# A transformer layer on eight cores: layernorm squares given to GpSimd, and every other gate-weight cast to VectorE

## What is computed

```python
def attn(x):                     # 16 heads of 64
    q = phi(heads(x @ Wq.T + bq)); k = phi(heads(x @ Wk.T + bk))   # phi = elu + 1
    v = heads(x @ Wv.T + bv)
    kv = einsum('bhtd,bhtm->bhdm', k, v)
    z = 1.0 / (einsum('bhtd,bhd->bht', q, k.sum(axis=2) + EPS) + EPS)
    return (q @ kv * z) @ Wo.T + bo
def ffn(x):                      # hidden 3072, int32 weights times 1/127
    return (silu(x @ wg.T) * (x @ wu.T)) @ wd.T
x = layernorm(x + attn(x))
x = layernorm(x + ffn(x))
```

## Time and profile before

| | us |
|---|---|
| median of the two timed runs | 5167.56 |
| these runs | 5112.57 and 5222.55 |
| the profiled execution's time | 5038.7 |
| its span (core 2, the slowest; the eight are 5019.1 to 5037.2) | 5037.2 |
| TensorE busy | 3672.0 (73%) |
| VectorE busy | 1673.3 (33%) |
| ScalarE busy | 1295.7 (26%) |
| GpSimd busy | 29.8 (1%) |

### The profile page before, as it was taken

One profiled execution on the slowest core, in us unless ns is written; L12 is line 12 of the kernel. 1 busy time (PEld: TensorE's weight loads), 2 busy tenths in 40 slices (PEclk: granted clock), 3 DMA queues, 4 the chain that ended last, 5 costly groups with the idle time before them and its releaser, 6 DMA issues.

```text
span 5037.2 us, 43743 instructions; the slowest of 8 cores (5019.1 to 5037.2 us)
## 1 busy us (share of the span) xinstructions
PE 3672.0 (73%) x15184; PEld 1440.3 (29%) x15184; DVE 1673.3 (33%) x2411; ACT 1295.7 (26%) x2299; POOL 29.8 (1%) x52
## 2 busy tenths in 40 slices
PE   1577647777756866799965866699974877599992
PEld 0232213333312322244421322244431322144440
DVE  0113422223332134333333133333343134333334
ACT  2234421111132344211123244311113243411113
POOL 0000000000000000000000000000000000000000
PEclk9797668888878977899987977799996987799995
DMA  5100022222211000010102000010003000001001
GB/s 159 44 1 1 0 75 75 75 76 76 74 67 67 1 1 0 26 51 26 51 34 100 1 0 1 25 42 34 35 16 134 1 1 0 25 26 51 26 26 67
DMA packets 69677, 199.99 MB, mean 40 GB/s; under 512 B 4933, under 2 KB 4934, under 8 KB 60248
## 3 DMA queue, kind: packets, MB, share of 16 engines
q1 hardware_dynamic: 57656, 157.35, 9.0%
q10 hardware_dynamic: 11808, 39.85, 2.4%
HBM read 144.75 MB, written 52.43 MB: 39 GB/s over the span
## 4 chain that ended last, share of the span: by engine, by line
PE 58%; ACT 14%; DVE 13%; DMA 8%; issue 6%; POOL 1%; DVEq 0%; ACTq 0%; SPq 0%; POOLq 0%
PE ps L767 13%; PE ps L746 12%; PE ps L792 12%; PE ps L412 5%; PE ps L615 5%; PE ps L367 4%; DVE wstage L248 4%; DVE x L252 4%; DMA wstage_i<-wu 3%; DMA wstage_i<-wg 3%; ACT arena L187 2%; ACT arena L185 1%; ACT arena L537 1%; ACT arena L581 1%; DVE h_arena L778 1%
## 5 line engine op out<-in xcount | busy, mean ns | idle before, releaser
L746 PE MATMUL ps<-y_bf,arena 128*128 128x512 bf16 x3072 | 706.0, 388 | 141.7 <-POOL arena L715 95.8
L767 PE MATMUL ps<-y_bf,arena 128*128 128x512 bf16 x3072 | 704.9, 386 | 106.8 <-DVE arena L715 106.8
L792 PE MATMUL ps<-h_arena,arena 128*128 128x512 bf16 x3072 | 694.1, 379 | 35.5 <-DVE h_arena L778 35.5
L756 ACT ACTIVATE h_arena<-ps 128x512 bf16<-128x512 f32 x384 | 229.1, 597 | 1805.2 <-PE ps L746 1805.1
L778 DVE SCALAR_TENSOR_TENSOR h_arena<-ps,h_arena 128x512 bf16<-128x512 f32 x384 | 265.6, 692 | 1044.0 <-PE ps L767 1043.3
L804 DVE SCALAR_TENSOR_TENSOR x<-ps,x 128x512 f32<-128x512 f32 x768 | 530.7, 692 | 182.3 <-DVE x L804 91.1
L412 PE MATMUL ps<-wk_bf,arena 128*128 128x512 bf16 x1024 | 286.7, 428 | 299.3 <-ACT arena L435 179.4
L746 PEld LDWEIGHTS ps<-y_bf,arena 128*128 128x128 bf16 x3072 | 304.8, 99 | 529.6 <-issue 182.9
L767 PEld LDWEIGHTS ps<-y_bf,arena 128*128 128x128 bf16 x3072 | 303.5, 99 | 492.5 <-issue 143.4
L792 PEld LDWEIGHTS ps<-h_arena,arena 128*128 128x128 bf16 x3072 | 293.7, 98 | 420.2 <-issue 80.1
L524 PE MATMUL ps<-arena,wq_bf 128*128 128x512 bf16 x1024 | 283.9, 447 | 96.8 <-ACT arena L537 86.6
(11 more groups left out here) (78 smaller groups left out, 2445.6 us busy)
## 6 DMA issues: line engine op xcount, KB each, us to landing
x<-x SPq DMA_DIRECT2D x16, 2048.0 KB, 8.2
out<-x SPq DMA_DIRECT2D x16, 2048.0 KB, 7.7
arena<-stash_wg SPq DMA_DIRECT2D x18, 1024.0 KB, 5.0
arena<-stash_wd SPq DMA_DIRECT2D x18, 1024.0 KB, 7.2
arena<-stash_wu ACTq DMA_DIRECT2D x18, 1024.0 KB, 4.8
wstage_i<-wg SPq DMA_DIRECT2D x48, 256.0 KB, 3.1
wstage_i<-wd ACTq DMA_DIRECT2D x48, 256.0 KB, 2.9
wstage_i<-wu SPq DMA_DIRECT2D x48, 256.0 KB, 2.7
```

What stands on the lines that cost most here:

```text
L746: e.matmul(ps[b_][:, 0:512], slots[sl_][:, 512 * kk + 128 * gg:512 * kk + 128 * (gg + 1)], y_bf[:, T * kk + t_:T * kk + t_ + 512], start=( ...
L756: e.activation(h_arena[:, 512 * gg:512 * (gg + 1)], ps[b_][:, 0:512], AF.Silu, scale=S127), inc=act)
L767: e.matmul(ps[b_][:, 0:512], slots[sl_][:, 512 * kk + 128 * gg:512 * kk + 128 * (gg + 1)], y_bf[:, T * kk + t_:T * kk + t_ + 512], start=( ...
L792: e.matmul(ps[b_][:, 0:512], slots[sl_][:, 1024 * ss + 128 * mm:1024 * ss + 128 * (mm + 1)], h_arena[:, 512 * ss:512 * (ss + 1)], start=(s ...
```

## The change

Two things are changed.

1. In `emit_layernorm` the square is made by GpSimd, as a product of the x32 piece with itself, in place of ScalarE's activation. ScalarE's copy now counts its semaphore on its own, GpSimd's stream has the same two waits as ScalarE's (x32 complete, scratch pair free), and TensorE waits for both engines. Ahead of LN2 GpSimd's stream gets the waits on the slot semaphores and on TensorE that ScalarE's has.
2. In batch 0's weight conversion, steps 1, 3, 5 and 7 of wg are cast by VectorE, steps 0, 2, 4 and 6 by GpSimd as before.

```diff
--- before.py
+++ after.py
@@ -183,12 +183,16 @@
                 p.wait("scalar", dve, src_ready_dve)
                 p.wait("scalar", pe, hist[m % npair])
                 p.op("scalar", lambda e, mm=m, t_=t0, d_=sa: e.copy(
-                    d_[:, :], x32[:, T * mm + t_:T * mm + t_ + 512]))
-                p.op("scalar", lambda e, mm=m, t_=t0, d_=sb_: e.activation(
+                    d_[:, :], x32[:, T * mm + t_:T * mm + t_ + 512]), inc=act)
+                cst = act.n
+                p.wait("gpsimd", dve, src_ready_dve)
+                p.wait("gpsimd", pe, hist[m % npair])
+                p.op("gpsimd", lambda e, mm=m, t_=t0, d_=sb_: e.tensor_mul(
                     d_[:, :], x32[:, T * mm + t_:T * mm + t_ + 512],
-                    AF.Square), inc=act)
-                cst = act.n
+                    x32[:, T * mm + t_:T * mm + t_ + 512]), inc=pool)
+                sq = pool.n
                 p.wait("tensor", act, cst)
+                p.wait("tensor", pool, sq)
                 p.op("tensor", lambda e, mm=m, d_=sa: e.matmul(
                     ps[ps_lo][0:1, 0:512], onesc[:, :], d_[:, :],
                     start=(mm == 0), stop=(mm == NCH - 1)))
@@ -651,8 +655,8 @@
                 p.wait(_eng, dve, p3_dve)
             stg_free = [None, None]
             stg_of = [0, 512]
-            conv_eng = {"wg": ("gpsimd", pool), "wu": ("vector", dve),
-                        "wd": ("scalar", act)}
+            conv_eng = {"wg": ("gpsimd", pool), "wg2": ("vector", dve),
+                        "wu": ("vector", dve), "wd": ("scalar", act)}
             load_q = {"wg": "sync", "wu": "sync", "wd": "scalar"}
             slot_map = [(0, 1, 2), (0, 1, 3), (0, 1, 2), (0, 1, 3),
                         (0, 1, 2), (0, 1, 3)]
@@ -678,8 +682,9 @@
                             slot_ready_k[slot_i][kk] = rdy
                         continue
                     qeng = load_q[wname]
-                    ceng, csem = conv_eng[wname]
                     for s in range(8):
+                        ceng, csem = conv_eng[
+                            "wg2" if (wname == "wg" and s % 2) else wname]
                         sub = 0 if wname != "wd" else 1
                         qsem = stg_sem[sub]
                         col = stg_of[sub]
@@ -815,7 +820,9 @@
 
             for _ss in slot_sem:
                 p.wait("scalar", _ss)
+                p.wait("gpsimd", _ss)
             p.wait("scalar", pe)
+            p.wait("gpsimd", pe)
             prev_apply = ffn_done
             prev_bc = pe.n
             ln2_apply = 0
```

## The result

The change makes the kernel slower by 0.75%: the ratio to the kernel before is 1.0075, with a 95% interval of 1.0059 to 1.0091. That is 38 us (30 to 46) of the 5038 us that the profiled execution before took. The forecast was +87 us, so the direction and the class (within 2%) are as forecast, and the size is less than half. Over all timed runs the medians are 5168.56 us after (5067.56 to 5436.77) and 5076.78 us before (5035.52 to 5416.6). Two states of the chip make these medians wide; the ratios in this text leave the disturbed runs out.

The account below looks back on a forecast made before the run. Exposed layernorm statistics and batch 0's weight conversion were taken to bound the kernel, with no engine full. Squares +43 and casts +44 gave +87 us, 5255 us on the 5167.56 median, range 5110 to 5370.

Parts of the forecast that it names:

- What bounds the kernel: Whole kernel: no engine full; each microsecond on the 32 layernorm statistics stretches moves the end by one; batch 0's conversion also bounds.
- The period P of the product: Layernorm statistics: GpSimd makes 8 products in a row, 1.28 us from one start to the next.
- two passes: GpSimd's square: priced at two passes at its cast's rate, 1.23 us, between bounds of 616 ns and 1.85 us.
- +43 us: Layernorm statistics: cost of moving the squares to GpSimd, 16 x (20.48 - 17.81).
- rival B: Layernorm statistics: product cheap, about 1.0 us; layernorms -13 us, with the casts +31, 5199 us; chance 0.15.
- The matmul pair: Layernorm statistics: TensorE's two matmuls behind each chunk, and the tail after the last, stay as before; stretch is eight periods.
- the loop over TensorE: LN1: with two scratch pairs, every second chunk waits for TensorE, 1.25 us, counting only when the product period is below that.
- The bound P under 0.94: Whole kernel: to end faster than before, the product's period must be under 0.94 us.
- The passages: Between batch 0's hidden blocks: second wg cast waits behind VectorE's tile 3 accumulations, delaying everything after; +44 us with cheaper casts.
- Rival C: Batch 0's weight conversion: wg delay is hidden, only -4.5 us stays; sum +38, 5206 us; chance 0.07.
- Rival A: Layernorm statistics: product dearer than 1.33 us, kernel slower by over 2%, 5401 us at 1.85; chance 0.38.
- GpSimd among others: GpSimd's operations beside VectorE: contention priced at nothing, since VectorE has no work during the statistics.

Follow-up runs that it names:

- e1: Kernel before with only the squares moved to GpSimd, all wg casts left there; ratio to before 0.9972, -14 us.
- e5: e1 with each square made twice on GpSimd, a wait between; ratio to before 1.0594, +299 us.
- e7: Kernel before with ScalarE's copies moved to VectorE and two more scratch pairs for LN1; ratio to before 0.9750, -126 us.
- e9: e1 with GpSimd's squares partly replaced by products of different float32 pieces (1265 ns), bf16 self-products (1040 ns) and plain copies; no whole-kernel time given.
- e10: e1 with every GpSimd product taken of two neighbouring x32 chunks, variance made a maximum and a sum; ratio to before 1.0172, +87 us.
- e2: Kernel before with only the four odd wg casts moved to VectorE, squares left on ScalarE; ratio to before 1.0092, +46 us.
- e3: e2 with only step 1 of wg cast by VectorE; ratio to before 1.0101, +51 us.

## Why the prediction was wrong in its size

- **What bounds the kernel: right.** The statistics are wholly exposed. e1, e5 and e7 change the 32 stretches by -11, +293 and -127 us (-14 for e1 over eight cores), and the whole kernel by -14, +299 and -126.
- **The period P of the product: the step that failed.** The prediction put it: "I take two passes, 1.23 us, nearest to the cast row, ... so P = 1.28". Measured are 1.038 us, 1.00 from start to start. The term "+43 us" is -14 in e1; the difference of 57 us is more than the whole miss of 49. VectorE's ratio of product to cast, which stood beside it and gave 998 ns, came nearer, and rival B, with P = 1.0, put the layernorms at -13 and the sum at +31; the trace has -13.4 and +33. It had a chance of 0.15. Both are near partly by luck. VectorE's 692 ns is a product of two different operands, and for such a product GpSimd's ratio to its own copy is 2.06 (1265 to 613 ns), not 1.62; the square has 1.69. And B had 6 us off LN1 and 7 off LN2, where the traces have 8.5, about half of it by the clock level, and 4.8. For two different operands the price was right (1.265 us in e9 and e10); I did not see that a square reads one operand twice and that this could be another price. The 0.05 us that I added between two products was also of the wrong sign: they overlap by 0.04.
- **The matmul pair "the same as before, and so is the tail": held in LN2, failed in LN1.** The sum has no clock level in it. Rival B expected the loop over TensorE to hold LN1 at 9.0 us for P = 1.0. It held some stretches at 9.5 to 10.4 and left others at 8.91, by the clock level of the matmul pairs (0.38 or about 0.6 us a matmul). The 1.25 us were the low level's number; at the high one, in the stretch shown above, the third copy follows 0.83 us behind the first product's end. With e10's P of 1.22 the forecast's own sum would be 16 x (19.52 - 17.81) = +27 us, and the stretches measure +52: there the tail is longer in LN2 as well (1.25 us for 0.83), and the scratch pairs bind in LN1. Whether they would at 1.28 no run shows. The bound P under 0.94 for a faster kernel leaves the loop out; with the 1.25 us it would be 0.84.
- **The passages: right.** +44 us forecast, +46 in e2 (36 to 56), 46 in the trace. e3 shows that the second cast alone makes it, as the prediction had it. What three cheaper casts more give back, 18 x 0.19 = 3.4 us by the prediction's own price, is not to be seen: e2 and e3 are 5 us apart in time, within their intervals, and 0.3 us in batch 0's feed-forward over eight cores.
- **Rival C: out.** The wu chain moved with wg's. **Rival A: out** for the square.
- **GpSimd among others: nothing against it.** The product is 1035 to 1042 ns in both scratch tiles and in all stretches of all cores; but VectorE was idle in every one, so a product beside a busy VectorE was not tested.

The Trainium skill (GPSIMD Engine Reference, section Performance versus the Vector engine) gives an estimate of 1.12 us from its time for 2048 elements, and another of 1.36 us from its ratio of 1.96 to VectorE. The rows differ from both: 1.04 for a square and 1.27 for two operands, which is 1.5 and 1.8 times VectorE's 692 ns. The measurement decides. Moving the squares to GpSimd still gained 14 us in e1, though GpSimd is the slower engine for them, because ScalarE had both of a chunk's operations before and they now run beside each other. Squares on VectorE were not tried.

## What to carry to other kernels

An operation moved to another engine takes its place in that engine's stream: look first at what stands ahead of it there and when that ends, for here one late step of a load, cast, load chain cost as much as all four. Where a stretch is bound by one engine's operations in a row, spread them over the engines that are idle in it, and check what each costs on the engine it goes to; a price taken from another operation should be bounded by ratios between engines as well as by sums of passes, and the chance should follow. When two parts of a change have opposite signs, measure them apart: here the half worth keeping was hidden by the other.

## What was not expected of the hardware

- GpSimd multiplies a 128x512 piece by itself in 1.04 us, float32 or bf16 alike, but two different pieces in 1.27 us (float32) or 1.15 us (bf16), overlapping or not. A copy or cast with one input is 0.61 from float32 or int32.
- GpSimd's operations in a row start 0.04 us sooner than the one before ends by the record (1.04 long, 1.00 apart); a wait for its own semaphore between two makes that 1.18.
- Where TensorE's statistics matmuls ran at the high clock level in LN1 (granted clock 1.00, 0.38 us a matmul), the same two scratch pairs did not bind at 1.00 us a chunk; at the low level (0.57 over the stretch, about 0.6 us) they did, and with the longer tail cost up to 1.5 us a stretch (8.91 against 10.4).
